# Cross-attention and gated feed-forward: another interleaving of the three steps of a head, from head 2 of the feed-forward attention on

## What is computed

```
h = rms_norm(x)                                  # 448 x 512
q, k, v = h@wq+bq, h@wk+bk, h@wv+bv              # 16 query heads, 8 key/value heads, of 128
q, k = rope(q), rope(k)
att  = softmax(causal(q k^T / sqrt(128)))        # per head 448 x 448
x1   = x + (att v, all heads) @ wo               # 2048 -> 512
mlp  = (silu(h2@w_gate) * (h2@w_up)) @ w_down    # h2 = rms_norm(x1)
```

## Time and profile before

| | us |
|---|---|
| median of 3 timed runs | 1527.26 (1526.75 to 1528.58) |
| the profiled execution, its own time | 1524.64 |
| span of that execution in the trace | 1522.9 |
| attention of the second layer, first score to last output product | 1249.31 to 1392.8 |

### The profile page before, as it was taken

One profiled execution on the slowest core, in us unless ns is written; L12 is line 12 of the kernel. 1 busy time (PEld: TensorE's weight loads), 2 busy tenths in 40 slices (PEclk: granted clock), 3 DMA queues, 4 the chain that ended last, 5 costly groups with the idle time before them and its releaser, 6 DMA issues.

```text
span 1522.9 us, 41381 instructions
## 1 busy us (share of the span) xinstructions
PE 1497.2 (98%) x16220; PEld 1186.7 (78%) x16220; DVE 1182.6 (78%) x1884; ACT 715.8 (47%) x1458; POOL 688.5 (45%) x727
## 2 busy tenths in 40 slices
PE   8999999999999999999999999999999999999997
PEld 6777777777777777777777777777777787778997
DVE  6765788888888888888888888888887686554986
ACT  5874444444444444444444444444445124655431
POOL 3543344454444454444444444544445692114752
PEclk9999999999999999999999999999999999999999
DMA  8961121211111221112221112121125524010000
GB/s 262 346 207 60 39 63 52 77 56 50 56 54 59 67 66 50 56 50 62 62 70 50 56 50 62 58 75 50 56 87 154 196 111 167 28 56 29 1 1 25
DMA packets 70199, 121.04 MB, mean 79 GB/s; under 512 B 21840, under 2 KB 36528, under 8 KB 68608
## 3 DMA queue, kind: packets, MB, share of 16 engines
q1 hardware_dynamic: 69312, 117.54, 23.9%
q0 software_dynamic: 832, 2.75, 0.7%
HBM read 89.93 MB, written 30.34 MB: 79 GB/s over the span
## 4 chain that ended last, share of the span: by engine, by line
PE 89%; DVE 5%; ACT 3%; issue 1%; DMA 1%; POOL 1%; ACTq 0%; DVEq 0%; POOLq 0%
PE ps L1535 21%; PE ps L1536 19%; PE ps L1537 18%; PE ps L1691 10%; PE ps L1654 6%; PE ps L1625 3%; PE ps L1596 3%; PE ps L1660 2%; PE ps L1900 2%; PE ps L1917 2%; PE ps L1909 1%; PE ps L1664 1%; DMA q_dram<-q_turned 1%; DVE rec L1163 1%; PE ps L1636 0%
## 5 line engine op out<-in xcount | busy, mean ns | idle before, releaser
L547 POOL TENSOR_TENSOR ctx_lo<-ctx_raw,ctx_hi 128x472 fp32r<-128x472 f32 (+1 forms) x62 | 112.8, 1819 | 192.8 <-ACT ctx_hi L780 192.8
L1163 DVE RECIPROCAL rec<-ps 128x224 f32<-128x224 f32 x128 | 198.3, 1549 | 1.1 <-PE ps L1691 0.9
L581 POOL TENSOR_TENSOR prob_img<-prob 128x448 f32<-128x448 f32 x93 | 107.9, 1160 | 149.3 <-ACT prob L845 149.3
L1152 DVE TENSOR_REDUCE top<-ps 112x4 f32<-112x1028 f32 x128 | 156.2, 1220 | 0.0
L1151 DVE TENSOR_REDUCE top<-ps 112x4 f32<-112x472 f32 x128 | 83.1, 649 | 72.9 <-PE ps L1625 72.9
L1654 PE MATMUL ps<-q_all,k_all 32*128 32x112 f32 (+1 forms) x3072 | 125.2, 274 | 0.0
L1535 PE MATMUL ps<-w_v_img_hi,ctx_hi 128*128 128x512 f32 x256 | 107.4, 419 | 0.0
L1535 PE MATMUL ps<-w_k_img_hi,ctx_hi 128*128 128x512 f32 x256 | 107.1, 418 | 0.0
L843 ACT ACTIVATE prob<-ps 119x448 f32<-119x448 f32 x96 | 52.4, 546 | 114.8 <-PE ps L1654 114.8
L1654 PEld LDWEIGHTS ps<-q_all,k_all 32*128 32x128 f32 (+1 forms) x3072 | 105.4, 184 | 0.0
L1536 PE MATMUL ps<-w_k_img_lo,ctx_hi 128*128 128x512 f32 x256 | 101.1, 395 | 0.0
(11 more groups left out here) (358 smaller groups left out, 4410.7 us busy)
## 6 DMA issues: line engine op xcount, KB each, us to landing
ctx_raw<-in_ctx_dram SPq DMA_DIRECT2D x32, 748.0 KB, 4.2
xh_dram<-xh SPq DMA_DIRECT2D x32, 448.0 KB
xc<-in_xT_dram SPq DMA_DIRECT2D x28, 256.0 KB, 4.5
q_dram<-q_turned SPq DMA_DIRECT2D x28, 256.0 KB, 4.6
q_all<-q_dram SPq DMA_DIRECT2D x32, 224.0 KB, 3.1
out_dram<-out_sb SPq DMA_DIRECT2D x32, 224.0 KB, 2.3
xh<-in_x_dram SPq DMA_DIRECT2D x31, 224.0 KB, 2.9
proj<-in_x_dram SPq DMA_DIRECT2D x21, 256.0 KB, 5.1
```

Source lines behind the costliest of these rows:

```text
L547: nc.gpsimd.tensor_tensor(ctx_lo[:, :, cols], ctx_raw[:, :, cols], ctx_hi[:, :, cols].bitcast(F32), ALU.subtract).then_inc(ctx_lo_done, 1)
L581: nc.gpsimd.tensor_tensor(prob_img[:, g % 2], image[:, 0, :], image[:, 1, :], ALU.add).then_inc(img_summed, 1)
L1152: nc.vector.tensor_reduce(rows[:, :, 2 * g + 1], ps[0:L, 2:6, TAIL:CTX], AX.X, ALU.max).then_inc(s_done, 1)
L1163: nc.vector.reciprocal(rec[:], bank[:, 2:4]).then_inc(norm_step, 1)
```

## The change

It touches the order of instructions on three queues and nothing else: no instruction is added or removed.

- **PE**, from head h = 2 on (k = 4h): turn(k-3), att(k), weigh(h-2), att(k+1), turn(k-2), att(k+2), first half of output_T(h-2), turn(k-1), second half of it, turn(k), att(k+3). `weigh` thus stands behind the first score tile of the head and not ahead of it; the turns c3 and c0 stand between the halves and behind them; the score tile c3 is last.
- **ACT** follows: evac(k-3), exp(k), attn_rounded(h-2), exp(k+1), evac(k-2), exp(k+2), wo_rounded(h-1), evac(k-1), evac(k), exp(k+3). The evacuation of tile c2 stands behind exp of c1, that of c3 and c0 behind exp of c2. The small `gate_exp` goes into head 6.
- **DVE**: at c0 and c3 scale_probs(k-1) comes ahead of the maximum of tile k; at c1 and c2 it stays behind. This holds from k = 4 on.

```diff
--- before.py
+++ after.py
@@ -1046,32 +1046,53 @@
                     act.wait_ge(down_step, j - 2)
                 nc.scalar.activation(m_hi[:, j % 3, :], m_prod[:, j % 2, :], ACT.Copy).then_inc(m_hi_done, 1)
 
-            for k in range(FH * NC + LAG + 2):
-                if k % NC == 0 and k >= 2 * NC:
-                    attn_rounded(k // NC - 2)
-                if LAG <= k < FH * NC + LAG:
+            def prob_exp(k):
+                c = k % NC
+                n_keys = (c + 1) * L
+                act.wait_ge(top_ready, k + 1)
+                if k < AMONG:
+                    act.wait_ge(head_ready, NHEAD - 2 * AMONG + k + 1)
+                if k > LAG:
+                    act.wait_ge(pT_full, k - LAG)
+                nc.scalar.activation(prob2[:, k % (LAG + 1), 0:n_keys], ps[0:L, 4 + k % 2, 0:n_keys], ACT.Exp, bias=neg_top[:, c:c + 1],
+                                     accum_out=prob_sum[:, c:c + 1]).then_inc(prob_ready, 1)
+
+            for k in range(2 * NC):
+                if k >= LAG:
                     turn_evac(k - LAG)
-                if k < FH * NC:
-                    c = k % NC
-                    n_keys = (c + 1) * L
-                    act.wait_ge(top_ready, k + 1)
-                    if k < AMONG:
-                        act.wait_ge(head_ready, NHEAD - 2 * AMONG + k + 1)
-                    if k > LAG:
-                        act.wait_ge(pT_full, k - LAG)
-                    nc.scalar.activation(prob2[:, k % (LAG + 1), 0:n_keys], ps[0:L, 4 + k % 2, 0:n_keys], ACT.Exp, bias=neg_top[:, c:c + 1],
-                                         accum_out=prob_sum[:, c:c + 1]).then_inc(prob_ready, 1)
-                if k == 24:
+                prob_exp(k)
+                if k == NC + 2:
+                    wo_rounded(0)
+            attn_rounded(0)
+            prob_exp(2 * NC)
+            turn_evac(2 * NC - 3)
+            for h in range(2, FH):
+                k = NC * h
+                if h >= 3:
+                    turn_evac(k - 3)
+                    prob_exp(k)
+                    attn_rounded(h - 2)
+                if h == 6:
                     act.wait_ge(gate_step, NC)
                     nc.scalar.activation(gate_e[:], sel_score[:], ACT.Exp, scale=-1.0).then_inc(gate_exp, 1)
-                if k % NC == 2 and 1 <= k // NC <= FH:
-                    wo_rounded(k // NC - 1)
-                if k == FH * NC + LAG:
-                    act.wait_ge(att_full, FH * NC)
-                    act.wait_ge(ring_loaded[0], 48)
-                    act.wait_ge(ring_loaded[1], 32)
-                    gate_up_rounded(0)
-                    gate_up_rounded(1)
+                prob_exp(k + 1)
+                turn_evac(k - 2)
+                prob_exp(k + 2)
+                wo_rounded(h - 1)
+                turn_evac(k - 1)
+                turn_evac(k)
+                prob_exp(k + 3)
+            turn_evac(FH * NC - 3)
+            attn_rounded(FH - 2)
+            turn_evac(FH * NC - 2)
+            turn_evac(FH * NC - 1)
+            wo_rounded(FH - 1)
+            act.wait_ge(att_full, FH * NC)
+            act.wait_ge(ring_loaded[0], 48)
+            act.wait_ge(ring_loaded[1], 32)
+            gate_up_rounded(0)
+            gate_up_rounded(1)
+            attn_rounded(FH - 1)
 
             for kc in range(KC):
                 at = FH + FKV + KC + kc
@@ -1437,10 +1458,13 @@
 
             for k in range(FH * NC + LAG + 3):
                 c = k % NC
+                sooner = c in (0, 3) and k >= NC
+                if sooner and k <= FH * NC:
+                    scale_probs(k - 1)
                 if k < FH * NC:
                     dve.wait_ge(att_full, k + 1)
                     nc.vector.tensor_reduce(neg_top[:, c:c + 1], ps[0:L, 4 + k % 2, 0:(c + 1) * L], AX.X, ALU.max, negate=True).then_inc(top_ready, 1)
-                if 1 <= k <= FH * NC:
+                if 1 <= k <= FH * NC and not sooner:
                     scale_probs(k - 1)
                 if k < 2:
                     rope(NHEAD - AMONG + k)
@@ -1936,21 +1960,32 @@
                     last.then_inc(o_step, 1)
 
             pe.wait_ge(consts2, 2)
-            for k in range(FH * NC):
-                if k % NC == 0 and k >= 2 * NC:
-                    weigh(k // NC - 2)
+            for c in range(AMONG):
+                att(c)
+                project_head(NHEAD - AMONG + c)
+            turn_probs(0)
+            for k in range(NC, 2 * NC):
                 att(k)
-                if k < AMONG:
-                    project_head(NHEAD - AMONG + k)
-                if k >= LAG:
-                    turn_probs(k - LAG)
-                if k % NC == 2 and 2 * NC <= k < FH * NC - NC:
-                    output_T(k // NC - 2)
-                elif k == FH * NC - 2:
-                    output_T(FH - 3, first)
+                turn_probs(k - LAG)
+            weigh(0)
+            att(2 * NC)
+            turn_probs(2 * NC - 3)
+            for h in range(2, FH):
+                k = NC * h
+                if h >= 3:
+                    turn_probs(k - 3)
+                    att(k)
+                    weigh(h - 2)
+                att(k + 1)
+                turn_probs(k - 2)
+                att(k + 2)
+                output_T(h - 2, first)
+                turn_probs(k - 1)
+                output_T(h - 2, second if h < FH - 1 else range(2, 3))
+                turn_probs(k)
+                att(k + 3)
+            turn_probs(FH * NC - 3)
             weigh(FH - 2)
-            turn_probs(FH * NC - 3)
-            output_T(FH - 3, range(2, 3))
             turn_probs(FH * NC - 2)
             output_T(FH - 3, range(3, KC))
             turn_probs(FH * NC - 1)
```

## The result

The changed kernel takes **1531.68 us** (median of 9 runs, 1530.79 to 1534.03), the kernel before 1527.26 beside it (9 runs, 1524.65 to 1528.58): 1.0032 of before, 95% interval 1.0022 to 1.0042. It is slower, by 4.4 us, where 2.0 were forecast and "no difference" was called likeliest. The profiled execution took 1531.29, with a span of 1529.6.

What follows compares the result with a forecast made beforehand. The prediction took PE, busy 98% of the span, to bound the kernel. Regular heads +0.6, start +1.1 and end +0.3 gave +2.0 us on 1527.26, so 1529.3 us, range 1526.2 to 1531.8.

Steps and rivals of the forecast that it cites:

- Part 1: In each regular head, spreading the turns ends PE's waits for evacuations of bank 6, a gain of 0.42 us.
- Part 2: In each regular head, with `weigh` later, the first output product waits 0.47 us for DVE and ACT.
- The second tie: In regular heads, c3's turn might wait for c2's evacuation behind exp of c1: 2.00 against 2.0 us, wait taken as 0.
- The first rival: In the regular heads the helpers' path is shorter and PE sets a period of 7.51: 1523.3 us, chance 0.08.
- Part 3: At head 2, the pattern's start, DVE's sooner scaling of tile 7 and later turns delay PE: +1.1 us (0.4 to 2.1).
- Part 4: In the last head, c0's turn waits for c3's evacuation behind exp of c2 and `wo_hi`: +0.3 us (0 to 0.6).
- the second rival: In regular heads, c3's turn does wait for c2's evacuation, 0.2 us per head: 1531.7 us, chance 0.30.

Runs made afterwards that it cites:

- DVE's plain order: The changed kernel with DVE back in its old order, the maximum always ahead of the scaling; PE's order stays new: 1526.73 us, 0.9996 of before.
- the changed kernel with filler: The changed kernel plus 8 and 14 unused PE products ahead of two waiting instructions of head 2: 1527.93 us, later 1528.39 us.
- DVE's order alone: The kernel before with only DVE's new order (scaling ahead of the maximum at c0 and c3), PE and ACT as before: 1528.82 us, 1.0014 of before.
- the best order without filler: The changed kernel with scaling sooner only at c3, from head 3 on, and ACT evacuating c3 ahead of `wo_hi`: 1524.47 us, 0.9984 of before.

## Why the prediction was wrong

By its own steps, each against the stage at full clock:

- **Part 1 (0.42 go): right.** No turn of c2 or c3 waits in the regular heads.
- **Part 2 (0.47 come): the path right, its size too large.** From the mask product of c3 (1299.36) to the first output product (1303.48) are 4.12 us, where the sum said 4.26; PE gets there in 3.80, as the sum said. The wait is 0.32. Most of the difference of 0.14 is the last handoff: from the start of `attn_lo` (1302.80) to the product are 0.68, where the sum had 0.62 + 0.16. The weight load shows 0.53, since the last load had ended at 1302.96, ahead of its mask product: of the two, the product's start is what moves the head. What I left out is PE's own price for **cutting the output in two**. A first product behind a turn has 0.28 to the next one (1305.14 to 1305.42), or 0.31 behind the wait, others 0.20, and there are now two such per head: twelve products with no wait take 2.65 (1303.48 to 1304.82 and 1305.14 to 1306.45) where before they took 2.53. That is some 0.1 per head. -0.42 + 0.32 + 0.10 = 0.00, which is what the period shows: 7.93 and 7.93. Two slips of 0.1 to 0.15 met each other; the forecast of +0.05 per head was near by luck as well as by working.
- **The second tie (taken at 0): right**, and the rival that it breaks, the only one with a time near the measured 1531.68, is wrong: c3's turn doesn't wait in the regular heads (once, by 0.16, in the last). The time met that rival's for another reason.
- **The first rival, the waits simply go: wrong**, though half of it was to be had. With DVE's plain order the period is 7.72.
- **Part 3 (+1.1): the delay right in size.** The turn of tile 6 starts 22.75 us behind the first score; the prediction's 1271.92 is 22.61 behind it. The scaling of tile 7 took 1.06 us beside POOL's rotation (1271.23 to 1272.36), as expected. The first output product is 0.90 late where the sum had 0.73; it took 1272.14 for the old start, which was 1272.06. The turn of tile 7 adds some 0.4, as expected. With full clock the score of tile 13 is 1.3 late.
- **Part 4 (+0.3): right.** 0.27 come behind the regular heads. The turn that waits is c0 of the last head, for the evacuation of head 14's c3, which stands behind `wo_hi`:

```profile
1385.62 0.28 PE L1933 MATMUL ps<-ident,rows 112*112 112x112 f32 x1 [0.30 <-ACT normed L1023]
```

The sum for the order, +2.0, stands against 1.56 measured. By that alone the forecast of no measurable change would have held: 1528.8 us, 1.0010; the changed kernel with filler gave 1.0010 and 1.0002, both intervals within 0.2%. The measured 1531.68 lies just inside the range given, but its upper end was the second rival's time, so that is luck.

**The step that failed is part 3's pricing of the wait in head 2**: it counted the wait's length and what it hides, and took for granted that PE goes on afterwards as fast as before. It does not always: behind the waits of 1.19 and 1.61 us PE's granted clock fell to 0.50, for which the sum has no term. Of three profiled executions of the changed kernel two ran some 3.5 us behind that wait at half the granted clock, for 1.66 us; of two of the kernel before, none. The filler shows that the idle stretch is what brings it: same order, same times of the helpers, no half clock in two profiles, medians lower by 1.3 (1529.23 and 1527.93, on different chips) and by 2.2 us (side by side), mean granted clock back to that of the kernel before. The earlier trace rows already showed PE waiting 0.81 and 0.71 there; a change that adds about a us of idleness to such a place needs a term for the clock, of 0 to 1.7 us.

What this doesn't settle is the 1.9 us in the MLP, though the prediction said that any change outside 1260 to 1393 us would prove it wrong. It is there in two of the three profiles of the changed kernel, the two with the half clock, and in none of the eleven others, among them two with half clock in head 2 (DVE's order alone, and the best order without filler). With the order at 1.56, the clock at 1.66 and the MLP at 1.9, an execution that has all three is 5.1 us longer, and one with the order alone 1.56; the medians of the three comparisons (+4.4, +2.2, +3.3) lie between. Order and clock together are 3.2, so at least 1.2 of the 4.4 are shown by no experiment. That the two come together may be chance; how one would cause the other no run here shows.

## What to carry to other kernels

A product stream cut in two pays its slower first product twice (here 0.1 us per head). When a consumer moves forward on one engine, look at what the other engines do ahead of the step that feeds it: here DVE scaled c3 ahead of the maximum of c0, and with the two exchanged 0.2 us per head come back, though DVE is busy only 77% of the time. Where a change adds idle time to PE at one place, add a term for the clock behind it, and test it with filler products, which leave the order alone. Of the orders tried, the one with only c2 scaled sooner and `wo_hi` behind the evacuation of c3 beats both kernels (0.9984, interval 0.9973 to 0.9995; with filler 0.9986, 0.9976 to 0.9995). And measure a small change by the distance between two instructions that frame it, not by the whole.

## What the hardware showed

- **Half clock behind an idle stretch, in some executions only.** With the same waits (1.19 and 1.61 us) the granted clock fell to 0.50 in two executions of the changed kernel and stayed at 1.00 in the third. With idle times of 1.20 and 0.71 (DVE's order alone) it fell in the one execution profiled, with 0.82, 0.65 and 0.55 in one of three, with those of the kernel before (0.81 and 0.52) in none of three. The Trainium skill (TensorE: Matmul & The Clock Gate, Part 1) says that a gate halves the clock of an idle PE and that the moment at which the clock rises to full differs between runs of one kernel. The trace agrees on the half, with 0.59 and 0.55 in the two stretches behind the wait in one execution; that the fall, too, comes in one execution and not in another (1.00) is this case's own.
- **Two speeds of the same product stream at full clock.** In the MLP the 128x448 products of two executions follow each other by 0.2067 us, of the others by 0.2027, for over 100 us on end, with the granted clock at 1.00 in both. The first and fourth of four products in a row, first at the lower speed, then at the higher:

```profile
1459.97 0.37 PE L1560 MATMUL ps<-hT_lo,gate_up_hi 128*128 128x448 f32 x1
...
1460.59 0.37 PE L1560 MATMUL ps<-hT_lo,gate_up_hi 128*128 128x448 f32 x1
```

```profile
1458.89 0.36 PE L1560 MATMUL ps<-hT_lo,gate_up_hi 128*128 128x448 f32 x1
...
1459.49 0.36 PE L1560 MATMUL ps<-hT_lo,gate_up_hi 128*128 128x448 f32 x1
```

  Three steps take 0.62 and 0.60. What sets one or the other is open.
- **A stage repeats to 0.03 us, the whole moves by 5.** The stage took 143.34, 143.32 and 143.35 us in three executions of the old order, while the time of the whole ran from 1524.5 to 1529.8 for the kernel before on one chip. Counted along ACT's instructions, the 14 profiled executions lie up to 3.4 us apart by 181 us, and up to 1202 us these distances then stay the same to within 0.4. In five of the 14, of the old order and of new ones, all on one chip, the granted clock falls to about a half between 156 and 164 us, in code that no edit touched.
